# Statistics matmuls two steps behind the convolution instead of one, input loads issued one step later, and two staging tiles instead of four

## The reference

```python
K = _s4_kernel(Lambda, p, q, B, Ct, step, L)
n = 2 * L
y = irfft(rfft(u, n=n) * rfft(K, n=n), n=n)[..., :L] + D[0] * u
x = _layernorm(x + y)
base_out = einsum('bsi,oi->bso', x, W) + b
gates = softmax(einsum('bsi,ei->bse', x, Wr))
proj_r = einsum('bsi,eri->bser', x, A)
lora_out = einsum('bser,eor->bseo', proj_r, Bm)
x = _layernorm(x + base_out + einsum('bse,bseo->bso', gates * 2.0, lora_out))
```

## Time and profile before

| what | value |
|---|---|
| median of 7 runs | 1861.78 us |
| lowest of 7 runs | 1859.85 us |
| the profiled execution | 1860.63 us |
| its span (slowest core, from its first to its last instruction) | 1859.6 us |
| the eight cores' spans | 1840.6 to 1859.6 us |
| convolution of pass 0, first copy to last square on ACT | 263.75 to 331.25 us |
| the same of passes 1, 2 and 3 | 735.89 to 806.24, 1089.85 to 1162.48, 1444.95 to 1516.60 us |
| PE busy / ACT busy / DVE busy, share of the span | 74% / 16% / 19% |

### The profile page before, as it was taken

One profiled execution on the slowest core, in us unless ns is written; L12 is line 12 of the kernel. 1 busy time (PEld: TensorE's weight loads), 2 busy tenths in 40 slices (PEclk: granted clock), 3 DMA queues, 4 the chain that ended last, 5 costly groups with the idle time before them and its releaser, 6 DMA issues.

```text
span 1859.6 us, 15494 instructions; the slowest of 8 cores (1840.6 to 1859.6 us)
## 1 busy us (share of the span) xinstructions
PE 1375.4 (74%) x5908; PEld 566.5 (30%) x5908; DVE 348.2 (19%) x598; ACT 298.2 (16%) x588; POOL 59.3 (3%) x83
## 2 busy tenths in 40 slices
PE   0155557059977768669999985799999669999960
PEld 0025522013323223223444431144444212444420
DVE  2331000050000002343100050530000515100025
ACT  0032236100000001630000045000000550000000
POOL 3000001000000000000000000000000000000000
PEclk9999998578988888878999998799999878999985
DMA  4001026931999993343534307073351162624204
GB/s 83 13 6 12 1 13 93 198 116 27 198 197 205 195 199 110 60 167 149 214 147 147 113 1 203 23 271 149 123 190 37 23 203 91 248 114 180 92 1 181
DMA packets 72928, 222.83 MB, mean 120 GB/s; under 512 B 10821, under 2 KB 60085, under 8 KB 68470
## 3 DMA queue, kind: packets, MB, share of 16 engines
q0 software_dynamic: 58544, 154.10, 34.1%
q1 hardware_dynamic: 14310, 67.73, 10.3%
HBM read 205.32 MB, written 67.43 MB: 147 GB/s over the span
## 4 chain that ended last, share of the span: by engine, by line
PE 57%; DMA 13%; ACT 9%; DVE 8%; another core or an unknown queue 7%; issue 4%; POOL 1%; SPq 0%; DVEq 0%; ACTq 0%; POOLq 0%
PE ps L942 41%; DMA wtb<-WT 7%; ACT uTb L110 3%; ACT r1b L110 3%; DMA uTb<-uT 2%; DVE bnbuf L105 2%; PE ps L900 2%; PE ps L902 2%; PE ps L946 2%; PE ps L949 1%; DMA o<-outf 1%; ACT carry L110 1%; PE ps L282 1%; DVE g L105 1%
## 5 line engine op out<-in xcount | busy, mean ns | idle before, releaser
L942 PE MATMUL ps<-wtb,r1b 128*128 128x512 bf16 x3968 | 896.1, 385 | 60.2 <-DVE wtb L105 60.2
L942 PEld LDWEIGHTS ps<-wtb,r1b 128*128 128x128 bf16 x3968 | 382.3, 99 | 566.4 <-issue 138.0
L110 ACT CAST scr<-ps 128x512 bf16<-128x512 f32 x64 | 37.5, 586 | 975.3 <-PE ps L949 824.0
L105 DVE CAST scr<-ps 128x512 bf16<-128x512 f32 x64 | 44.2, 691 | 594.3 <-PE ps L949 590.6
L105 DVE BATCH_NORM_STATS2 bnbuf<-scr 128x6 f32<-128x512 bf16 x128 | 88.9, 694 | 13.4 <-DVE scr L105 0.7
L804 PE MATMUL ps<-r1b,onescb 128*1 128x512 bf16 x128 | 50.6, 396 | 45.3 <-ACT uTb L110 42.5
L110 ACT ACTIVATE uTb<-r1b 128x512 bf16<-128x512 bf16 x128 | 80.6, 630 | 12.8 <-ACT r1b L110 1.5
L110 ACT CAST r1b<-ps 128x512 bf16<-128x512 f32 x128 | 75.0, 586 | 26.8 <-PE ps L834 13.7
L105 DVE TENSOR_TENSOR wtb<-wtb,eyeb 128x128 bf16<-128x128 bf16 x32 | 7.2, 225 | 363.2 <-DMA wtb<-WT 360.4
L823 PE MATMUL ps<-carry,pstat 128*128 128x512 bf16 x64 | 27.0, 422 | 62.5 <-DMA uTb<-uT 42.8
L105 DVE TENSOR_SCALAR outf<-scr,bnagg,sigcol 128x1024 f32<-128x1024 bf16 x64 | 52.0, 813 | 109.7 <-DMA o<-outf 107.7
(11 more groups left out here) (588 smaller groups left out, 756.2 us busy)
## 6 DMA issues: line engine op xcount, KB each, us to landing
wtb<-wscr POOLq DMA_DIRECT2D x24, 4096.0 KB, 13.7
wtb<-WT POOLq DMA_DIRECT2D x8, 4096.0 KB, 49.4
wscr<-wtb SPq DMA_DIRECT2D x8, 4096.0 KB, 21.0
o<-outf SPq DMA_DIRECT2D x64, 512.0 KB, 3.1
uTb<-uT POOLq DMA_DIRECT2D x16, 1024.0 KB, 14.7
g<-cvb_re POOLq DMA_DIRECT2D x1, 1024.0 KB, 7.4
g<-cvb_im POOLq DMA_DIRECT2D x1, 1024.0 KB, 10.9
catb<-CatA POOLq DMA_DIRECT2D x1, 288.0 KB, 7.5
```

What stands on the lines that cost most here:

```text
L105: t = sy.inc("V", fn(*a, **kw))
L110: t = sy.inc("S", fn(*a, **kw))
L942: T.matmul(ps[bi][0:128, 0:512], r1b[:, it * TT + tb * 128: it * TT + (tb + 1) * 128], wtb[par][:, it * 512:(it + 1) * 512], start=(it == ...
```

## The change

Three edits.

- `stage8` has two tiles and two semaphores instead of four, and the tile is chosen by `half` instead of by a running number modulo 4.
- In step `c` the statistics matmuls are those of step `c - 2` instead of `c - 1`. After step 15 come `st_mm(14)` and `st_mm(15)`.
- Load 2 is issued at the end of step 5 instead of 4, and load 3 at the end of step 9 instead of 8.

```diff
-                  "YB", "YS0", "YS1", "YS2", "YS3", "YO0", "YO1", "YW0", "YW1"]:
+                  "YB", "YS0", "YS1", "YO0", "YO1", "YW0", "YW1"]:
...
-                stage8 = [sb2(f"stage8{i}", [16, 512], F32) for i in range(4)]
-                stage_tok = [None, None, None, None]
+                stage8 = [sb2(f"stage8{i}", [16, 512], F32) for i in range(2)]
+                stage_tok = [None, None]
...
-                        sg = (2 * c + half) % 4
+                        sg = half
...
-                if c > 0:
-                    st_mm(c - 1)
+                if c > 1:
+                    st_mm(c - 2)
...
-                if c == 4:
+                if c == 5:
                     uq_tok[2] = u_dma(t, 2, [sy.tok("T"), sy.tok("S"), sy.tok("V")])
-                if c == 8:
+                if c == 9:
                     uq_tok[3] = u_dma(t, 3, [sy.tok("T"), sy.tok("S"), sy.tok("V")])
...
+            st_mm(14)
             st_mm(15)
```

## The result

The changed kernel takes 1877.34 us (median of 14 runs) beside 1863.04 us for the kernel before (35 runs): ratio 1.0067, 95% interval 1.0052 to 1.0082, that is 10 to 15 us slower. Forecast was 1880 us, range 1870 to 1886. Measured once more, in a group of runs where the kernel before took 1878.4 us, the ratio is 1.0036 (1.001 to 1.0062). So the sign and the range held. The profiled execution took 1876.06 us, its slowest core is now core 0, span 1875.0 us.

The account below looks back on a forecast made before the run. ACT was taken to set the steps' pace, with loads 2 and 3 deciding when steps 8 and 12 start. Load 2 3.57 + load 3 14.52 + clock 1.36 = 19.45 us on 1860.63 gave 1880 us, range 1870 to 1886.

Parts of the forecast that it names:

- ACT sets the pace and the statistics wait is spare time: Convolution steps: ACT needs 3.57 us per step, PE 2.86, so removing PE's 0.71 us wait at L804 gains 0.
- Load 3 is on the path in each pass: PE already waits for load 3 before step 12, so issuing it a step later adds 14.52 us over four passes.
- Load 2 is held by DVE in passes 1 to 3, so its slip costs nothing there: Load 2's issue waits for DVE's `ln2_stats`, 5.8 us after step 5: 0 in passes 1 to 3.
- Clock term in pass 1: PE's restart behind load 3 in pass 1 was expected to turn slow, at 1.2 GHz: + 1.36 us.
- Staging tiles: Tile reuse after two copies instead of four has 2.6 us or more to spare: 0; tripled writes would wait.
- The convolution and the weights of pass 0 move together: In pass 0 weight blocks issued behind load 3 slip with the convolution by 7.14 us, counted once.
- pass 0 catches up: Rival: less crowding in the shared weight stream makes good the later start, removing 7.14 us: 1873 us; chance 0.06.
- the statistics order with the staging: Statistics matmuls one step further back and two staging tiles: each taken as 0 in the forecast.
- The bound of 11 us: Largest gain allowed for the statistics order: 0.71 us in the two steps behind each of 8 loads.

Follow-up runs that it names:

- kernel 3: The kernel before with loads 2 and 3 issued one step later in passes 1 to 3 alone; ratio 1.0078 to the kernel before, some 15 us.
- kernels 7 and 8: The kernel before (7) and the changed kernel (8), loads 2 and 3 no longer waiting for DVE; ratios 0.9849 and 0.9949 to the kernel before.
- kernel 4: The kernel before with two staging tiles and two semaphores instead of four, nothing else; ratio 1.0007 to the kernel before.
- kernel 2: The kernel before with loads 2 and 3 issued one step later in pass 0 alone; ratio 1.0062 to the kernel before, some 12 us.
- kernel 6: The kernel before with only loads 2 and 3 issued one step later, beside the changed kernel on one chip; 1901.5 us, ratio 1.0111 to the kernel before.
- Kernels 9 and 10: The changed kernel with four staging tiles again (9), and late loads with two staging tiles, statistics one step behind (10); both ratio 1.0101 to the kernel before.
- kernels 1 to 10: Follow-up kernels; those without their own line: 1, the kernel before with late loads alone, ratio 1.0123; 5, the changed kernel measured again, 1.0036.

## Why the prediction was right, and where it wasn't

- *ACT sets the pace and the statistics wait is spare time*: right. Period 3.57 us, wait moved to L823.
- *Load 3 is on the path in each pass*: right. Its waits grew to 7.4 to 7.8 us on the slowest core, and kernel 3 with late loads in passes 1 to 3 alone costs 15 us by itself. That the two waits of the earlier trace rows put down to ACT were the load's fits: with the load later, both grew and are put down to the DMA.
- *Load 2 is held by DVE in passes 1 to 3, so its slip costs nothing there*: right, shown by kernels 7 and 8. Without DVE's wait the changed kernel falls 19.0 us behind.
- *Clock term in pass 1*: the slow restart came (0.59 us), but the term was read from core 3, one core of eight. Behind load 3 of passes 1 to 3 PE had a slow stretch in 10 of 24 cases before (two of three on core 3) and in 24 of 24 after; behind the loads of pass 0, for which no clock term was forecast, in 8 of 16 and 16 of 16. Nor did all waits of 2.9 us or longer end slow at once: on core 4 one of 3.07 us was followed by five matmuls at 2.4 GHz and then by some at 1.2 GHz. In the mean, steps 12 and 13 together took 9.2, 8.9 and 9.8 us in the three passes before and 13.5, 13.4 and 13.3 us after. So it is luck in part that the sums agree as well as they do (passes 1 to 3: 11.2 us for 12.3; the convolution of pass 0: 7.3 for 7.1): more restarts turned slow than the forecast had, and the rows don't separate what each cost from what the later issue cost. The page that the prediction cites for this term (the Trainium skill, "TensorE: Matmul & The Clock Gate", What's actually happening) says of a kernel's start that the number of slow matmuls varies from run to run; in these traces it varies at restarts too, from 6 to 13 behind the late loads of the changed kernel.
- *Staging tiles*: nothing by themselves, shown by kernel 4 within its interval (2 us less to 4 us more would go unseen). For writes three times as long the prediction's wait is 126.79 + 7.32 - 131.90 = 2.2 us and not 2.3; nothing hangs on it.
- *"The convolution and the weights of pass 0 move together"*: this step failed for the changed kernel. The convolution grew by 7.3 and the weights were issued 7.0 us later, as forecast, but the stream behind them took 9.3 us less, and nothing of it reached pass 1. The rival *pass 0 catches up* gave 1873, + 12.3 us; measured are + 12.5 us by the ratio. But its reason, less crowding after a later start, isn't confirmed: with late loads alone pass 0 does not catch up. Pass 1 begins 13.2 us later in kernel 2 than in kernel 3 and 11.3 us later in kernel 6 than in kernel 7, each pair on one chip.
- The forecast's 19.45 us is thus near what the late loads cost alone (23 and 21 us by the ratios 1.0123 and 1.0111), but its parts are not right: pass 0 was put too low (7.1 us for 11 to 13), and the term that I set to 0, the statistics order with the staging, was mis-sized: together with late loads it gave 15 us back on one chip. That 1880 us lies 3 us from the measured 1877.3 is luck in part, since these two errors have opposite signs. The bound of 11 us that I had given for a gain looked for it at PE's waits behind the loads, where 2 us of it are; the rest is in the flight of the weight blocks.

Still open is why. The same bytes go out by the same 8 instructions, with the same waits behind them. Kernels 9 and 10, late loads with one of the two other edits each, can be read either way. Two rivals stand untested: that the fewer staging tiles change where later tiles lie in memory, and that PE's order changes how the cores' streams meet. What would tell is all five kernels, before, changed, late loads alone, 9 and 10, in one group, with profiles of several executions of each.

## What to carry to other kernels

A wait on the engine that you look at is worth something only if the engine that sets the pace has idle time too; here, of 45.3 us of PE's waiting, 35 moved to other instructions and the rest, at the ends of the passes, stayed. A deeper skew has a price where later reads of a buffer delay the load that overwrites it: look at what the load waits for, not at where it is written, and wait for no engine that doesn't touch the buffer, which alone was worth 28 us. A stage bound by transfers that all cores make at once need not shift as a block: 7 us more were forecast for pass 0, and pass 1 then began 2 us earlier in the changed kernel and 13 us later in kernel 2. Bound such a term from both sides.

## What the runs showed of the hardware that was not expected

The stream of the same 8 weight blocks, 4 MB each once they are in bf16 (they are read in fp32), took 387 to 412 us (mean of the cores) in the twelve profiles of before, changed and kernels 1 to 10, which all issue it by the same rule, and on one chip 394.0 and 393.9 us in the two kernels with the whole change against 406.2 and 409.5 us in the two without. After waits of 2.57 and 2.62 us PE came back once at 1.2 and once at 2.4 GHz. Over the eight cores of the kernel before, the shortest wait behind a load with a slow first matmul was 2.11 us (core 1, pass 3). The longest with a fast one was 3.07 us, and there the clock fell while PE was at work: the granted clock was 1.00 for the first five matmuls, 0.50 from 788.4 to 791.8 us and 1.00 after that (core 4, pass 1):

```profile
787.18 0.38 PE L823 MATMUL ps<-carry,pstat 128*128 128x512 bf16 x1 [3.07 <-DMA uTb<-uT]
...
788.25 0.47 PE L832 MATMUL ps<-uTb,band1b 128*128 128x512 bf16 x1
788.52 0.63 PE L833 MATMUL ps<-uTb,band0b 128*128 128x512 bf16 x1
...
791.30 0.61 PE L823 MATMUL ps<-carry,pstat 128*128 128x512 bf16 x1
791.70 0.45 PE L824 MATMUL ps<-uTb,win_sb 128*128 128x512 bf16 x1
791.98 0.38 PE L825 MATMUL ps<-uTb,win_sb 128*128 128x512 bf16 x1
```
